# The recurrent stage's rows gathered by quarters and turned in 32x32 blocks on VectorE instead of by TensorE transposes

## The reference

```python
x = x + _L0_ffn_ref(_L0_cond_ref(x, cond_1024, ...), ...)       # two layers of experts, 32 batches
# _L1_cond_ref: experts chosen by a hash of the token id
out_pad = concatenate([expert_out.reshape(E * C, D), zeros((1, D))])
y = out_pad[slot].reshape(B, T, D)                               # slot: which row of the experts' output
r = sigmoid(einsum('btd,ed->bte', xr, w_recept))
x2 = r * y
# _L1_ffn_ref: a recurrence over the 32 batches, each step on 128 tokens of 512 columns
def step(c, xt):
    ft = sigmoid(xt @ wf.T + c @ uf.T + bf)
    it = sigmoid(xt @ wi.T + c @ ui.T + bi)
    gt = tanh(xt @ wc.T + c @ uc.T + bc)
    return ft * c + it * gt, None
h = tanh(einsum('tbi,oi->tbo', x2, wo) + c_final @ uo.T + bo)
x = x + h
```

## Time and profile before

| | |
|---|---|
| median of 3 runs | 2510.55 us (2509.78 to 2514.25) |
| span of the profiled execution, first to last instruction | 2502.9 us |
| TensorE busy | 2451.8 us (98%) |
| VectorE, ScalarE, GpSimd busy | 1148.3, 897.2, 551.4 us |
| mean granted TensorE clock | 0.996 of full speed |

### The profile page before, as it was taken

One profiled execution on the slowest core, in us unless ns is written; L12 is line 12 of the kernel. 1 busy time (PEld: TensorE's weight loads), 2 busy tenths in 40 slices (PEclk: granted clock), 3 DMA queues, 4 the chain that ended last, 5 costly groups with the idle time before them and its releaser, 6 DMA issues. The chain is left out here.

```text
span 2502.9 us, 40913 instructions
## 1 busy us (share of the span) xinstructions
PE 2451.8 (98%) x12556; PEld 2046.1 (82%) x12557; DVE 1148.3 (46%) x1771; ACT 897.2 (36%) x1459; POOL 551.4 (22%) x498
## 2 busy tenths in 40 slices
PE   8999999999999899999999989999999999999999
PEld 4778888888899688888888878998978888888877
DVE  5655555325343344344434356766643333332356
ACT  2233333216555222222222246666642222222234
POOL 1100000002222276666657510000011111111100
PEclk9999999999999999999999999999999999999999
DMA  8698898317466433363343266665641011110025
GB/s 297 210 329 310 301 318 317 141 44 269 150 238 223 172 120 111 114 255 108 113 171 127 92 235 230 239 227 222 241 141 43 25 34 30 29 34 25 25 101 185
DMA packets 135988, 412.81 MB, mean 165 GB/s; under 512 B 29843, under 2 KB 34419, under 8 KB 119394
## 3 DMA queue, kind: packets, MB, share of 16 engines
q1 hardware_dynamic: 108626, 314.20, 35.3%
q0 software_dynamic: 19072, 61.66, 7.7%
q10 hardware_dynamic: 8208, 35.88, 3.7%
HBM read 558.71 MB, written 144.80 MB: 281 GB/s over the span
## 5 line engine op out<-in xcount | busy, mean ns | idle before, releaser
L99 PE MATMUL s_g<-wx_hi,s_x_hi 128*128 128x512 f32 x512 | 203.4, 397 | 2.3 <-DVE s_x_lo L2306 1.6
L101 PE MATMUL s_g<-wx_hi,s_x_lo 128*128 128x512 f32 x512 | 200.2, 391 | 0.0
L100 PE MATMUL s_g<-wx_lo,s_x_hi 128*128 128x512 f32 x512 | 199.5, 390 | 0.0
L2019 DVE TENSOR_TENSOR s_w_lo<-s_w_raw,s_w_hi 128x1024 fp32r<-128x1024 f32 x124 | 146.4, 1222 | 75.3 <-ACT s_w_hi L1948 73.7
L99 PE MATMUL s_g<-s_u,s_c_hi 128*128 128x512 f32 x384 | 152.8, 398 | 1.6 <-PEq L1833 1.6
L101 PE MATMUL s_g<-s_u,s_c_lo 128*128 128x512 f32 x384 | 149.9, 390 | 0.0
L100 PE MATMUL s_g<-s_u,s_c_hi 128*128 128x512 f32 x384 | 149.5, 389 | 0.0
L99 PE MATMUL s_h_ps<-s_x_hi,s_w_hi 128*128 128x256 f32 x512 | 144.9, 283 | 1.7 <-DVE s_x_lo L2044 1.7
L101 PE MATMUL s_h_ps<-s_x_hi,s_w_lo 128*128 128x256 f32 x512 | 144.9, 283 | 0.0
L100 PE MATMUL s_h_ps<-s_x_lo,s_w_hi 128*128 128x256 f32 x512 | 144.9, 283 | 0.0
L2205 POOL DMA_INDIRECT s_y<-mid_hash_out,first_rec x32 | 31.6, 986 | 475.4 <-DMA mid_hash_out<-s_o 392.8
(11 more groups left out here) (411 smaller groups left out, 6814.0 us busy)
## 6 DMA issues: line engine op xcount, KB each, us to landing
s_half<-mid_w ACTq DMA_DIRECT2D x124, 2048.0 KB
s_w_raw<-in_w SPq DMA_DIRECT2D x64, 512.0 KB, 6.2
mid_w<-s_x_grp SPq DMA_DIRECT2D x32, 1024.0 KB, 5.8
mid_w<-s_pool_b SPq DMA_DIRECT2D x32, 1024.0 KB, 4.9
s_half<-mid_w SPq DMA_DIRECT2D x32, 1024.0 KB
s_w_raw<-in_w2h SPq DMA_DIRECT2D x16, 2048.0 KB, 7.4
s_w_raw<-in_w1h SPq DMA_DIRECT2D x15, 2048.0 KB, 7.4
mid_routed<-s_o_sb SPq DMA_DIRECT2D x72, 256.0 KB
```

Source lines behind the costliest of these rows:

```text
L99: pe.matmul(out, a_hi, w_hi, start=first, stop=False, skip_group_check=True)
L100: pe.matmul(out, a_hi, w_lo, start=False, stop=False, skip_group_check=True)
L101: return pe.matmul(out, a_lo, w_hi, start=False, stop=last, skip_group_check=True)
L2019: dve.tensor_tensor(lo[:, c], raw[:, c], hi[:, c], ALU.subtract).then_inc(S[name + "_lo"], 1)
```

## The change

A tile `y` is gathered not as 128 rows of 512 columns but as four lists of 128 quarter rows of 128 columns. The rows of `hash_out` and `r` are written with their columns in another order (`by_quarter`: ScalarE's copies out of PSUM write the order g, k, a of column k*128 + 32g + a), so that quarter g of a row has the columns that belong to partitions 32g to 32g + 31 of the turned tile. Partition 32g + t gets in its four gathers the quarters g of tokens t, 32 + t, 64 + t and 96 + t. Then a turn of every 32x32 block gives the whole turned tile, and VectorE does that in one instruction (`turn_quarters`). In detail:

- `stage_shared` makes a table `hash_quarter` (4 x slot + g; four VectorE instructions of 128x32) and stores it to DRAM, behind the store of `rec`, by a second DMA of 128 x 32 pieces of 16 bytes. Those of `rec` have 24 bytes.
- SP loads a batch's numbers by four DMAs of 32 partitions, four bytes a piece, and `r` by four of 32 partitions, 512 bytes a piece, in place of one each.
- GpSimd starts four gathers where there was one, writes the product back into `y`, waits for the turn, and copies the turned tile to `x2t` (ScalarE did that out of PSUM).
- VectorE turns `y` into `x2`, at the head of its step j, ahead of the gates of j - 2. `x_hi` and `x_lo` are made from `x2`.
- TensorE's transposes of `x2` are gone.

```diff
@@ -99,6 +99,34 @@
     return pe.matmul(out, a_lo, w_hi, start=False, stop=last, skip_group_check=True)
+def load_by_quarters(eng, dst, rows, sem):
+    for g in range(P // 32):
+        eng.dma_start(dst[32 * g:32 * g + 32].rearrange("t (s c) -> t s c", c=P),
+                      rows[:, g * P:(g + 1) * P].rearrange("(s t) c -> t s c", t=32)).then_inc(sem, 16)
+def in_order(row):
+    return row.rearrange("p (k g a) -> p k g a", k=DC, g=4)
+def by_quarter(row):
+    return row.rearrange("p (g k a) -> p k g a", g=4, k=DC)
+def load_places(eng, dst, places, sem):
+    for g in range(P // 32):
+        eng.dma_start(dst[32 * g:32 * g + 32, 0:4], places[:, g].rearrange("(s t) -> t s", t=32),
+                      allow_slow_non_contiguous=True).then_inc(sem, 16)
+def turn_quarters(dve, dst, src):
+    return dve.transpose(dst.rearrange("p k (s t) -> p k s t", t=32), src.rearrange("p (s k a) -> p k s a", s=4, a=32))
...
@@ -329,6 +359,7 @@
             pool.dma_start(d["rec"].rearrange("i p c -> p i c"), rec[:]).then_inc(S["rec_out"], 16)
+            pool.dma_start(d["hash_quarter"].rearrange("i p g -> p i g"), hash_quarter[:]).then_inc(S["quarter_out"], 16)
...
@@ -523,6 +554,8 @@
                 op(dve.tensor_copy(rec[:, :, SLOTH], slot))
+                for g in range(4):
+                    op(dve.tensor_scalar(hash_quarter[:, :, g], slot, 4.0, float(g), ALU.mult, ALU.add))
...
@@ -1580,7 +1613,7 @@
                 wait_for(act, S["r_out"], i * 16)
-                act.activation(r[:], r_bank(i), ACT.Copy).then_inc(S["r_ready"], 1)
+                act.activation(by_quarter(r[:]), in_order(r_bank(i)), ACT.Copy).then_inc(S["r_ready"], 1)
...
@@ -1912,11 +1945,12 @@
                     sp.dma_start(staged[:], ins["gate_w"][0:NST].rearrange("u p n -> p u n")).then_inc(S["u_in"], 16)
-                    sp.dma_start(first_rec[:], d["rec"][0]).then_inc(S["rec_in"], 16)
+                    sp.wait_ge(keep["early"]["quarter_out"], 16)
+                    load_places(sp, first_rec, d["hash_quarter"][0], S["rec_in"])
                     for m in range(2):
                         sp.wait_ge(S[f"tx{m}"], EH)
                     sp.dma_start(first_c[:], ins["in_c"].partition_broadcast(P)).then_inc(S["c_in"], 16)
-                    sp.dma_start(first_r[:], d["r"][0]).then_inc(S["r_in"], 16)
+                    load_by_quarters(sp, first_r, d["r"][0], S["r_in"])
...
@@ -1977,7 +2011,7 @@
                     wait_for(act, S[f"o_out{m}"], e * 16)
-                    act.activation(o_sb[m][:], o_ps[m][:], ACT.Copy).then_inc(S[f"o_ready{m}"], 1)
+                    act.activation(by_quarter(o_sb[m][:]), in_order(o_ps[m][:]), ACT.Copy).then_inc(S[f"o_ready{m}"], 1)
...
@@ -2169,10 +2203,10 @@
                 wait_for(sp, S["x2"], i)
-                sp.dma_start(rec[:], d["rec"][i]).then_inc(S["rec_in"], 16)
-                sp.dma_start(r[:], d["r"][i]).then_inc(S["r_in"], 16)
-            sp.wait_ge(S["y_in"], 16)
+                load_places(sp, rec, d["hash_quarter"][i], S["rec_in"])
+                load_by_quarters(sp, r, d["r"][i], S["r_in"])
+            sp.wait_ge(S["y_in"], 64)
...
@@ -2200,15 +2234,17 @@
             def fetch(i):
-                wait_for(pool, S["rec_in"], i * 16)
-                wait_apart(pool, S["x2"], i)
-                pool.indirect_dma_start(y[:], None, d["hash_out"],
-                                        bass.IndirectOffsetOnAxis(rec[:, SLOTH:SLOTH + 1].bitcast(U32), 0)
-                                        ).then_inc(S["y_in"], 16)
-                pool.wait_ge(S["y_in"], i * 16 + 16)
+                wait_for(pool, S["rec_in"], i * 64)
+                wait_apart(pool, S["x2t"], i)
+                for s in range(4):
+                    pool.indirect_dma_start(y[:, s * P:(s + 1) * P], None, d["hash_out"].rearrange("s (g c) -> (s g) c", c=P),
+                                            bass.IndirectOffsetOnAxis(rec[:, s:s + 1].bitcast(U32), 0)
+                                            ).then_inc(S["y_in"], 16)
+                pool.wait_ge(S["y_in"], i * 64 + 64)
                 pool.wait_ge(S["r_sig"], i + 1)
-                wait_for(pool, S["tx"], i)
-                pool.tensor_tensor(x2[:], y[:], r[:], ALU.mult).then_inc(S["x2"], 1)
+                pool.tensor_tensor(y[:], y[:], r[:], ALU.mult).then_inc(S["x2"], 1)
+                pool.wait_ge(S["x2t"], i + 1)
+                pool.tensor_copy(x2t[:, i].rearrange("p k n -> p (k n)"), x2[:]).then_inc(S["kept"], 1)
...
@@ -2219,15 +2255,13 @@
             def r_sigmoid(i):
-                wait_for(act, S["r_in"], i * 16)
+                wait_for(act, S["r_in"], i * 64)
                 act.activation(r[:], r[:], ACT.Sigmoid).then_inc(S["r_sig"], 1)
 
             def x_parts(i, n, turn):
-                act.wait_ge(S["tx"], i + 1)
-                act.activation(x2t[:, i], tx_ps[:], ACT.Copy).then_inc(S["x_raw"], 1)
-                act.wait_ge(S["x_raw"], i + 1)
+                act.wait_ge(S["x2t"], i + 1)
                 wait_apart(act, S["xpart"], (i - 1) * NG)
-                act.activation(x_hi[:, n], x2t[:, i], ACT.Copy).then_inc(S["x_hi"], 1)
+                act.activation(x_hi[:, n], x2_turned, ACT.Copy).then_inc(S["x_hi"], 1)
...
@@ -2247,7 +2281,7 @@
                                    ACT.Copy).then_inc(S["wo_hi"], 1)
-                    act.wait_ge(S["x_raw"], NB)
+                    act.wait_ge(S["kept"], NB)
...
@@ -2275,9 +2309,15 @@
         def _(dve):
+            def turn_x(i, n, turn):
+                dve.wait_ge(S["x2"], i + 1)
+                wait_for(dve, S["kept"], i)
+                wait_for(dve, S["x_lo"], i)
+                turn_quarters(dve, x2_turned, y[:]).then_inc(S["x2t"], 1)
             def x_lo_(i, n, turn):
                 dve.wait_ge(S["x_hi"], i + 1)
-                dve.tensor_tensor(x_lo[:, n], x2t[:, i], x_hi[:, n], ALU.subtract).then_inc(S["x_lo"], 1)
+                dve.tensor_tensor(x_lo[:, n], x2_turned, x_hi[:, n], ALU.subtract).then_inc(S["x_lo"], 1)
...
@@ -2323,7 +2363,7 @@
 
-            software_pipeline(dve, NB, [(2, before_output), (2, gates), (2, lambda i, n, turn: c_part(i + 1)), (0, x_lo_)], 2)
+            software_pipeline(dve, NB, [(0, turn_x), (2, before_output), (2, gates), (2, lambda i, n, turn: c_part(i + 1)), (0, x_lo_)], 2)
...
@@ -2409,19 +2442,10 @@
 
-            def turn_first(first):
-                def stage(i, n, turn):
-                    if first == (isinstance(i, int) and i == 1) and not (isinstance(i, int) and i == 0):
-                        turn_x(i, n, turn)
-                return stage
-            first_c_part([(G_G, range(DC)), (G_I, range(DC)), (G_F, range(DC // 2))])
-            turn_x(0, 0, 0)
-            first_c_part([(G_F, range(DC // 2, DC))])
+            first_c_part([(G_G, range(DC)), (G_I, range(DC)), (G_F, range(DC))])
             software_pipeline(pe, NB, [
                 (2, c_part), (1, x_part((0, 1))), (2, first_outputs), (2, lambda i, n, turn: turn_c(i + 1)),
-                (0, turn_first(True)), (1, x_part((2,))),
-                (0, turn_first(False))], 2)
+                (1, x_part((2,)))], 2)
```

More of the change, by code:

```diff
@@ L158, in stage_shared @@
                  "xt_in xt_hi xt_lo gu silu hmul h_hi h_lo mm2 o_ready ~o_out0 ~o_out1 one_hot list_ps list_sum hash_members hash_total_read hash_rank_read "
-                 "rank_read members rec_done part_in0 part_in1 part_hi part_lo ~part_out0 ~part_out1")
+                 "rank_read members rec_done ~quarter_out part_in0 part_in1 part_hi part_lo ~part_out0 ~part_out1")
         keep["early"] = S
@@ L205, in stage_shared @@
         rec = sb("rec", [P, NB, REC], I32)
+        hash_quarter = sb("hash_quarter", [P, NB, 4], I32)
+        d["hash_quarter"] = nc.dram_tensor("mid_hash_quarter", [NB, P, 4], I32, kind="Internal").ap()
         rec_f = rec[:].bitcast(FP32)
@@ L1934, in _ @@
             sp.wait_ge(S["o_out0"], 16 * EH)
-            sp.wait_ge(S["rec_in"], 16)
-            sp.wait_ge(S["r_in"], 16)
+            sp.wait_ge(S["rec_in"], 64)
+            sp.wait_ge(S["r_in"], 64)
         @block.scalar
@@ L2128, in stage_recurrent @@
         ps = lambda n, s, t=FP32: ctx.enter_context(nc.psum_tensor("s6_" + n, s, t))
-        S = sems(nc, ctx, "s6_", "params_in wo_in wo_hi wo_lo rec_in ~y_in r_in r_sig x2 tx x_raw x_hi x_lo xpart "
+        S = sems(nc, ctx, "s6_", "params_in wo_in wo_hi wo_lo rec_in ~y_in r_in r_sig x2 x2t kept x_hi x_lo xpart "
                  "gates added acted ig fc c tc c_hi c_lo late_in uo_in ct_ready const_ps const "
@@ L2152, in stage_recurrent @@
         x2 = sb("x2", [P, D])
+        x2_turned = x2[:].rearrange("p (k n) -> p k n", k=DC)
         ct = x2
         g_ps = [[ps(f"g{n}_{g}", [P, D]) for g in range(NG)] for n in range(2)]
-        tx_ps = ps("tx_ps", [P, DC, P])
         tc_ps = ps("tc_ps", [P, DC, P])
@@ L2348, in _ @@
         def _(pe):
-            def turn_x(i, n, turn):
-                pe.wait_ge(S["x2"], i + 1)
```

(4 more changed lines are left out.)

## The result

| | kernel before | changed kernel |
|---|---|---|
| median | 2511.71 us (2509.78 to 2514.25, 5 runs) | 2520.3 us (2518.95 to 2523.49, 5 runs) |
| ratio | 1 | 1.0040, 95% interval 1.0027 to 1.0052 |
| profiled span | 2502.9 us | 2517.3 us |

A forecast was written before the change was run, and what follows sets the result against it. TensorE was taken as the bound, with fetching hidden mid-stage but not at its head. Head +17.8, turns -14.9, clock +1.7 and store +6.0 made +10.6 us on 2510.55: 2521 us, range 2511.5 to 2528.

The forecast's parts named there:

- Turns: Recurrent stage: each TensorE turn removed saves 0.495 us; 30 outside the head give -14.9 us.
- Head: Start of the recurrent stage: TensorE waits about 4.7, 5.4 and 10.9 us; +17.8 us, two saved turns already taken off.
- The pitch: In the head, four gathers behind each other start 1.29 us apart.
- three rounds: In the head, three rounds of number load, gathers and product lie behind each other, where TensorE's work had covered them.
- Later steps: Recurrent steps after the head: VectorE's turn is hidden with 1.7 us to spare, a 12.8 us round fits 16.8; no cost.
- Clock: Behind the head's 10.9 us wait TensorE runs 3.4 us at half clock: +1.7 us, bounds 0 and 3.4.
- Store: Shared stage: the second table's store delays a weight part's load and TensorE waits: +6.0 us, bounds 0 and 11.4.
- hits harder: Rival, shared stage: the weight load waits for all of the second store, +16.0 us, 2527; chance 0.07.

The follow-up runs named there:

- spare turns: Changed kernel plus four TensorE transposes of a constant behind each tile's x matmuls, read by nobody: 2529.94 us, 1.0093 of the kernel before.
- second profiled execution: The changed kernel run once more, unchanged, on another chip: 2518.67 us, 1.0038 of the kernel before.
- over seven: The seven profiled executions with the second store of small pieces: from rec store to s_gate matmul 29.22 to 32.69 us, mean 30.5.
- the kernel with the store alone: Kernel before plus only the second table: its four VectorE instructions and its store behind the first table's; 2514.88 us, 1.0038 of the kernel before.
- the kernel with both tables by rows: Changed kernel, both tables stored in 128 pieces, VectorE's turn behind the gates, numbers of tiles 1 and 2 loaded a stage earlier, raw later: 2498.23 us, 0.9963.
- the kernel with the second store by rows: Changed kernel with the second table stored in SBUF order, 128 pieces of 512 bytes instead of 4096 of 16: 2513.27 us, 1.0021 of the kernel before.
- the kernel with the turn moved: Changed kernel with VectorE's turn of a tile behind the gates and c_lo of the tile two before: 2507.53 us, 0.9999 of the kernel before.

## Why the prediction was right

- **Turns.** 0.495 us each were forecast, 0.467 measured, -14.0 for -14.9. The spare turns show that it is TensorE's time.
- **Head.** +17.8 forecast, +16.7 measured, 15.8 in the second profiled execution. The pauses were 3.29, 2.83 and 10.96 us for 4.7, 5.4 and 10.9. The first two were forecast too long mainly because the rows of a 64 KB gather are there 2.62 us after its start (1863.94 to 1866.56), and I had taken the 3.59 us of 256 KB. This is the bound that the Trainium skill, "DMA: Bandwidth & Descriptors", Anatomy of one DMA, spoke for; by it 0.45 us would be saved, and the trace shows 0.97. The second was also shorter because TensorE came to it later: behind the 3.29 us wait its clock was at half from 1871.6 to 1874.6, and the 36 matmuls of tile 0 took 10.1 us for the 8.2 reckoned. The third agrees to 0.1 us by luck: both of its ends, 30.4 and 41.3 us after the first state matmul, came 1.4 to 1.5 us sooner than forecast. The pitch (1.25 to 1.31 for 1.29) and the turn (0.71 for 0.7) were right. The Trainium skill, "VectorE: DVE Perf Modes", The three transpose paths, has only a figure for a quarter of the size, and the estimate of 1.24 us from it doesn't hold here.
- **Its reason** was half right. The prediction named both the long rounds and the gates queued behind the turn, but put the loss down to "three rounds" that "now lie behind each other". With the order as it is, shorter rounds give back 7 to 8 us; with four gathers as they are, the order gives back 10.5. These are more together than the 16.7, since the late `c` needs both: the long rounds and the gates behind the turn.
- **Later steps.** Hidden, as said; the 1.7 us "to spare" was wrong as a limit, since 2.2 us more cost no step anything.
- **Clock.** 1.7 forecast; the first step took 2.24 us more than the others, 1.44 in the second execution and 0.98 to 2.20 in the other kernels that keep the long wait. The transposes of `c` took 1.11 us for 0.66, which is in the head. That a half clock costs nothing after the first wait held: TensorE then waited for tile 1 all the same.
- **Store.** +6.0 forecast; 8.7 in the profiled execution, 5.3 to 8.7 over seven, 6.6 on the mean. ScalarE waited 16.92 us for 14, TensorE 10.52 for 7.8. The forecast had the slow stretch go on for another 9 us at 86 GB/s; in the trace the 93 GB/s of the first 9 us become 168 and 159, and still the load comes only when the store is down (128.5 and 128.67; in the kernel with the store alone 125.8 and 126.12; in all seven within 0.6 us). So the step from the amount moved to the load's delay was wrong. What the traces show is nearer to the rival "hits harder", in which the load waits for all of the store, at nearly the price of the forecast; what in the DMA queues holds the load isn't shown.

In the medians the sum came out at +8.6 for +10.6, in the profiled spans at +14.4. That 2521 met 2520.3 so closely is in part luck: the store's term alone moves by 3.5 us between executions, and the errors of head and turns nearly cancel.

## What to carry to other kernels

A small table written to DRAM in another order than it has in SBUF costs by its pieces: write it in rows of SBUF and let the small loads do the reordering (the steps stayed at 16.85 us with such loads). Before work moves to an engine with idle time, look at what stands behind it in that engine's list while its input is late; here the average of 46% busy said nothing, and one changed line gave about 10 us. A pipeline's fetch that is hidden in the steady steps is bare in the first ones: count its rounds there by themselves.

## What was not expected of the hardware

- 4096 pieces of 24 bytes took 13.1 us to land, the same bytes in 128 pieces 2.2 us, and while they were under way all queues together moved 86 to 103 GB/s with the DMA engines 89 to 97% busy. The Trainium skill, "DMA: Bandwidth & Descriptors", Specifications, has 512 B as the least size for full rate. The traces agree in kind: 768 B and 512 B pieces were down after 2.3 and 2.1 us in the kernel with both tables by rows, 16 and 24 B ones not. Behind the small pieces of the first table the 512 B ones too took 12.4 us (the kernel with the second store by rows).
- One VectorE instruction turns all 32x32 blocks of a 128x512 fp32 tile in 0.71 us, as long as a plain pass (0.69).
- The fp32 copy of such a tile on GpSimd took 0.61 us, half of its product (1.26).
- In the 10.96 us wait TensorE's granted clock fell to half (1.2 GHz) at 1891.8, and came back at 1905.5, 5.9 us after TensorE had taken up work. Shorter waits had it or not: in the changed kernel the clock was at half from 1871.6 to 1874.6 behind the 3.29 us wait and stayed full behind the 2.83 us one (1.00 from 1882.91 to 1888.65); in the kernel with the turn moved a wait of 2.53 us had a fall of 3.4 us behind it.
